# A third bank for the scores of the last batch, with its output projections two steps later

## The chip, the cores and the metric

The kernel runs on one core of one Trainium2 chip. The metric is device time in microseconds (us) of one launch. Before the change the median of three runs is 540.99 us (540.56 to 542.72).

## The reference

Input x is 8 batches of 512 tokens with 256 features. Each batch goes through one attention layer with 16 heads of 16 features:

```
xn = layer_norm(x) * norm_w + norm_b
q, k, v = xn @ q_w + q_b, xn @ k_w + k_b, xn @ v_w + v_b      (heads of 16)
att = softmax over keys of (q . k + mask term)
y   = att @ v
h   = layer_norm(y, sb weights) * (1 + scale) + shift          (scale, shift from silu(cond) @ emb_w)
out = x + silu(h) @ out_w + out_b
```

## The kernel before, in words

**Tiling.** A batch b is worked in 16 steps t: four groups of four heads (g = t // 4), and in each group four chunks of 128 keys (c = t % 4). A step computes four score tiles of 128 keys x 512 queries, one a head. Such a tile is called a unit; unit u = 4t + h. ScalarE turns a unit into probabilities with one exp (`exp_unit`, L678), and in the next step the TensorE multiplies the four probability tiles with v and accumulates them into one bank (`pv_step`, L541, 8 matmul records a step). A unit's softmax needs its query's largest score beforehand, so six steps ahead of the scores the same products are made once more the other way round (`max_quad`, L490) and reduced by VectorE (`max_pair`, L854, two reductions a step). Once every four steps the maxima of a group are turned on TensorE (`max_turn`, L500), split in two bf16 parts by VectorE (`split_max`) and written by a DMA as extra rows of q.

**PSUM.** There are eight banks: two score banks (`st_ps`), four max banks (`mx_ps`, in two pairs), one for the probability-times-v sums (`pv_ps`) and one job bank (`job_ps`). Unit h of a step takes score bank h % 2, so a score matmul waits until the exp of two units before has read its bank. In the last batch (b = 7) no maxima are due after step 9, so from step 11 on (`WIDE_STEP`) the scores take four banks: two score banks and the second pair of max banks.

**Jobs.** The rest of the work stands in tables by step. A job (`job`, written to the job bank) is a projection, a v projection or half of an output projection (`outp`) of the batch before; half A is token chunk 0 of its pair of chunks, half Z is chunk 1, and after Z VectorE adds the residual and bias (L916, reads `job_ps` and `x_res`). A side job (`side`) is four transposes into the first max bank: `yturn i` turns group i of y, `hturn i` the normalised y. It waits until VectorE has reduced the first pair of max banks in that step (`max_done`). In the last batch the job table holds only `proj 3` in step 0 (its bank is read by ScalarE, L690, in step 1) and the four outp halves.

**Order on TensorE in one step:** scores 0 and 1, max turn, pv of the step before, max matmuls, scores 2 and 3, job, side job. In the wide steps scores 2 and 3 come ahead of pv. TensorE works in this order and stops at the first instruction whose wait is not met.

**Around the end.** After the last batch comes one more body (b = 8) with only the tail: the last pv step, the last y turn, layer norm of the last y, gate and output projection (`last_rows` of each engine; TensorE fills the wait with dummy matmuls, L434). SyncE's queue (SP) handles `out` stores of the outp results (L1290) and then, in body 8, the load of `x_res`, the residual input of the last batch, 512 KB (L1278). That load waits until both outp results of batch 6 have been added (`out_ready`), as they read the same buffer. GpSimd (POOL) adds the output bias to `x_res` (L1178) and only then, in its program order, computes the reciprocal root for the last layer norm (L1095, `last_norms`), which waits for VectorE's `y_vareps` (L987), and half of the normalised rows (L1099):

```
pool.wait_ge(res_loaded, 16 * b)
pool.tensor_tensor(x_res, x_res, ob_row, ADD)     # L1178
if last_body(b):
    last_norms()                                  # L1095, L1099
```

Of the kernel before, what the change touches and what calls it, by code (L numbers as in the profile page):

```python
# [33 lines left out]
B, T, D = 8, 512, 256  # L34
# [8 lines left out]
GH = 4  # L43
NG = HEADS // GH
GC = GH * HD
STEPS = NG * CH
UNITS = STEPS * GH
# [3 lines left out]
ST_BANKS = 2  # L51
# [19 lines left out]
A, Z, AZ = (0,), (1,), (0, 1)  # L71
# [11 lines left out]
SIDE = {1: ("yturn", 3, -1), 5: ("yturn", 0, 0), 7: ("hturn", 0, -1), 9: ("yturn", 1, 0),  # L83
        11: ("hturn", 1, -1), 13: ("yturn", 2, 0)}

LAST_JOBS = {0: ("proj", 3, 0, AZ), 9: ("outp", 0, -1, A), 10: ("outp", 0, -1, Z), 11: ("outp", 1, -1, A),
             12: ("outp", 1, -1, Z)}
LAST_SIDE = {1: ("yturn", 3, -1), 5: ("yturn", 0, 0), 6: ("hturn", 0, -1), 7: ("hturn", 1, -1),
             9: ("yturn", 1, 0), 13: ("yturn", 2, 0)}
LAST_LATE = {(1, 2): ("proj", 3, 0), (7, 2): ("hturn", 0, -1), (8, 2): ("hturn", 1, -1)}  # L90

WIDE_STEP = 11

TURNS = {2: 1, 6: 2, 10: 3, 14: 4}

# [18 lines left out]
def work_at(table, b, step):  # L114

    if step not in table or not job_exists(table[step][0], b, table[step][2]):
        return None
    kind, i, db = table[step][0:3]
    return (kind, i, b + db) + table[step][3:]


def of_loop(b, first, middle, last):

    return first if isinstance(b, int) and b == -1 else last if isinstance(b, int) and b == B - 1 else middle


def wide(b, t):

    return isinstance(b, int) and b == B - 1 and t >= WIDE_STEP


def job_at(b, step):

    if step < 0:
        b, step = b - 1, step + STEPS
    return work_at(of_loop(b, FIRST_JOBS, JOBS, LAST_JOBS), b, step)

# [21 lines left out]
def exists(batch):  # L159

    return not isinstance(batch, int) or 0 <= batch < B
# [9 lines left out]
def wait(engine, semaphore, count):  # L171

    if not isinstance(count, int) or count > 0:
        engine.wait_ge(semaphore, count)
# [10 lines left out]
def attention_layer(nc, x, cond, mask, norm_w, norm_b, q_w, q_b, k_w, k_b, v_w, v_b,  # L185
                    emb_w, emb_b, sb_w, sb_b, out_w, out_b, out):
    with ExitStack() as ctx:
# [3 lines left out]
        def psum(name, shape, dt=F32):  # L191
            return ctx.enter_context(nc.psum_tensor(name, shape, dt))

        def sem(name):
            return ctx.enter_context(nc.semaphore(name))
# [68 lines left out]
        st_ps = [psum(f"st_ps{i}", [P, T]) for i in range(ST_BANKS)]  # L264
        mx_ps = [psum(f"mx_ps{i}", [P, 2, T]) for i in range(PAIRS)]
        pv_ps = psum("pv_ps", [P, T])
        job_ps = psum("job_ps", [P, T])
# [47 lines left out]
        exp_done = sem("exp_done")  # L315
# [36 lines left out]
        def emptied(kind, i, batch):  # L352
            if kind == "proj":
                return part0_ready, NG * batch + i + 1
            if kind == "yturn":
                return y_ready, NG * batch + i + 1
            of = {"xturn": xt_ready, "vproj": v_plain_ready, "hturn": h_lin_ready, "outp": out_ready}[kind]
            return of, 2 * batch + i + 1
# [9 lines left out]
        def bank_freed(t, b):  # L368

            if isinstance(b, int) and b == -1:  # L370
                return {7: (xt_ready, 1), 8: (mask_col_ready, 1)}.get(t)
            if 0 not in job_at(b, t)[3]:
                return None
            for back in range(t - 1, t - STEPS, -1):
                if isinstance(b, int) and b == 0 and back < 0:
                    return None
                job = job_at(b, back)
                if job and 1 in job[3]:
                    return emptied(*job[0:3])
            return None  # L380
# [11 lines left out]
        last_ps = [[mx_ps[i][:, k, :] for k in range(KD)] for i in range(2)]  # L392
        last_out = [job_ps, st_ps[1]]

        wide_ps = [st_ps[0][:, :], st_ps[1][:, :], mx_ps[1][:, 0, :], mx_ps[1][:, 1, :]]

        def st_bank(b, t, h):

            return wide_ps[h] if wide(b, t) else st_ps[h % ST_BANKS][:, :]

        def last_body(b):

# [26 lines left out]
        def _(pe):  # L429
# [72 lines left out]
            def st_unit(b, t, h):  # L502
                if not exists(b):
                    return
                g, c = t // CH, t % CH
                if c == 0 and h == 0:

                    pe.wait_ge(max_filled[g], 2 * 16 * (b + 1))
                    if isinstance(b, int) and b == 0 and g == 0:

                        pe.wait_ge(cond_ready, 1)
                        pe.wait_ge(part0_ready, NG - 1)

                u = GH * t + h
                if wide(b, t) and t > WIDE_STEP:
                    pe.wait_ge(exp_done, UNITS * b + u - GH + 1)
                elif wide(b, t) and h >= ST_BANKS:
                    pe.wait_ge(max_done, PAIRS * STEPS * B)
                    pe.wait_ge(max_split, NG * B)
                else:  # L520
                    wait(pe, exp_done, UNITS * b + u - ST_BANKS + 1)
                pe.matmul(st_bank(b, t, h), k_rows[0:ROWS_ALL, g, h, c * P:(c + 1) * P],  # L522
                          q_rows[0:ROWS_ALL, g, h, :], start=True, stop=True).then_inc(st_ready, 1)

# [40 lines left out]
            def job(t, b):  # L565
                if not job_at(b, t):
                    return
                kind, i, d, halves = job_at(b, t)
                ps, freed = job_bank(kind, i, b), bank_freed(t, b)
                if freed:  # L570

# [60 lines left out]
            def body(b):  # L632
                for t in range(STEPS):
                    st_unit(b, t, 0)
                    st_unit(b, t, 1)
                    max_turn(b, t)
                    if wide(b, t):
                        st_unit(b, t, 2)
                        st_unit(b, t, 3)
                    pv_step(b, t)  # L640
                    max_quad(b, t)
                    if isinstance(b, int) and b == -1 and STEPS - MAX_LEAD <= t < STEPS - 1:

                        keep_warm(st_ps[1], WARM_MAX)
                    if not wide(b, t):
                        st_unit(b, t, 2)
                        st_unit(b, t, 3)
                    job(t, b)
                    side(t, b)
                    if isinstance(b, int) and b == -1 and t == TURN_STEP:  # L650
                        turn_cond()
                    if isinstance(b, int) and b == -1 and 0 <= t - EMBEDDING_STEP < 2 * KD:
                        embedding(t - EMBEDDING_STEP)
                    if isinstance(b, int) and b == -1 and t in WARM_FIRST:
                        keep_warm(pv_ps, WARM_FIRST[t])

                if last_body(b):
                    last_rows()
# [5 lines left out]
        def _(act):  # L664
# [5 lines left out]
            def exp_unit(b, t, h):  # L670
                if not exists(b):
                    return
                u = GH * t + h
                if h == 0:

                    wait(act, pv_done, STEPS * b + t - P_SLOTS + 1)
                act.wait_ge(st_ready, UNITS * b + u + 1)
                act.activation(probs[:, t % P_SLOTS, h, :], st_bank(b, t, h), ACT.Exp).then_inc(exp_done, 1)  # L678
# [640 lines left out]
```

## Time and profile before

| | us |
|---|---|
| median of three runs | 540.99 |
| the profiled execution's own time | 541.04 |
| its span, first to last instruction | 539.3 |
| TensorE busy | 513.1 |
| VectorE busy | 414.3 |
| ScalarE busy | 367.7 |
| GpSimd busy | 193.7 |
| mean granted TensorE clock | 0.994 |

Busy times are sums over the span. Busy matmul time is modelled, so the busy share of TensorE is not how near it is to its peak. The profiled execution's time lies 1.7 us over its span.

### The profile page before, as it was taken

To read this page: it belongs to the slowest core of one execution; us is meant where nothing else is said; L and a number is where in the kernel's file an instruction comes from. 1 tells how busy PE (TensorE), PEld (TensorE's weight loads), DVE (VectorE), ACT (ScalarE), POOL (GpSimd) and SP (SyncE) were. 2 spreads that over 40 slices of the span, in tenths; PEclk is the share of its full clock that TensorE was granted. 3 is DMA by queue.
4 is the path that set the end of the run, shared out by engine and by line. 5 is a ranking of instruction groups with operands and counts; after the bars stand their busy time and mean duration, and the time that the engine had idled before them with its cause. 6 is when DMAs were issued, how large, how long until landed. Compare 5 with 4: busy or idle time off the path is not lost.

```text
span 539.3 us, 10032 instructions
## 1 busy us (share of the span) xinstructions
PE 513.1 (95%) x2840; PEld 190.4 (35%) x2843; DVE 414.3 (77%) x661; ACT 367.7 (68%) x674; POOL 193.7 (36%) x240
## 2 busy tenths in 40 slices
PE   7698999899999999999999999999999999988987
PEld 3443333233334333433333333433333333422334
DVE  6587778887887878877887878878787877877625
ACT  2205777677776788577776877677776787666761
POOL 4535213535324333425225432525225433224011
PEclk9988999999999999999999999999999999999999
DMA  5643334242425334253425333243435323252011
GB/s 132 225 117 94 91 90 127 88 135 79 136 88 159 110 104 113 60 167 92 133 86 170 103 90 118 80 157 89 127 89 163 102 84 88 79 161 55 19 61 40
DMA packets 55050, 57.95 MB, mean 107 GB/s; under 512 B 12376, under 2 KB 42200, under 8 KB 55024
## 3 DMA queue, kind: packets, MB, share of 16 engines
q1 hardware_dynamic: 54480, 56.84, 35.6%
q10 hardware_dynamic: 544, 0.79, 0.5%
q8 instruction: 12, 0.20, 0.2%
q14 instruction: 14, 0.11, 0.1%
HBM read 36.35 MB, written 21.00 MB: 106 GB/s over the span
## 4 chain that ended last, share of the span: by engine, by line
PE 75%; ACT 9%; issue 6%; DVE 4%; DMA 2%; SPq 2%; ACTq 1%; DVEq 0%; POOL 0%; POOLq 0%
PE pv_ps L541 20%; PE st_ps L522 18%; PE mx_ps L490 11%; PE job_ps L579 8%; ACT probs L678 6%; PE job_ps L586 5%; PE job_ps L599 4%; PE mx_ps L624 3%; DVE negmax L854 2%; PE mx_ps L500 2%; ACT h_tanh L726 1%; PE mx_ps L629 1%; PE st_ps L434 1%; DMA qk_dram<-qk_parts 1%; SPq L1218 1%
## 5 line engine op out<-in xcount | busy, mean ns | idle before, releaser
L854 DVE TENSOR_REDUCE negmax<-mx_ps 128x2 f32<-128x1024 f32 x256 | 303.4, 1221 | 90.5 <-PE mx_ps L490 90.4
L678 ACT ACTIVATE probs<-st_ps 128x512 f32<-128x512 f32 x502 | 273.3, 600 | 112.8 <-PE st_ps L522 111.1
L522 PE MATMUL st_ps<-q_rows,k_rows 115*128 115x512 bf16 x502 | 158.1, 385 | 6.0 <-ACT probs L678 3.4
L541 PE MATMUL pv_ps<-probs,v_rows 128*32 128x512 f32 x1024 | 136.4, 605 | 0.6 <-ACT probs L678 0.6
L1111 POOL TENSOR_TENSOR qk_rest<-qk_full,qk_parts 128x512 f32<-128x512 f32 x31 | 35.9, 1159 | 142.3 <-ACT qk_parts L690 141.9
L490 PE MATMUL mx_ps<-k_rows,q_rows 51*128 51x512 bf16 x512 | 79.4, 384 | 6.2 <-DMA k_rows<-qk_dram 4.4
L522 PEld LDWEIGHTS st_ps<-q_rows,k_rows 115*128 115x128 bf16 x502 | 38.7, 97 | 109.9 <-ACT probs L678 77.2
L1120 POOL TENSOR_TENSOR qk_parts<-qk_rest,qk_parts 128x512 bf16<-128x512 f32 x31 | 36.0, 1163 | 101.6 <-DVE qk_parts L928 99.7
L579 PE MATMUL job_ps<-x_norm_t,w_qk 128*128 128x512 f32 x116 | 59.2, 603 | 0.0
L490 PEld LDWEIGHTS mx_ps<-k_rows,q_rows 51*128 51x128 bf16 x512 | 15.8, 94 | 112.1 <-issue 54.2
L541 PEld LDWEIGHTS pv_ps<-probs,v_rows 128*32 128x32 f32 x1024 | 20.1, 108 | 33.1 <-issue 27.9
L586 PE MATMUL job_ps<-w_v,x_norm_t 128*128 128x256 f32 x120 | 31.0, 381 | 0.0
L599 PE MATMUL job_ps<-w_o,h_t 128*128 128x256 f32 x112 | 28.6, 386 | 1.0 <-DVE out_sb L916 1.0
L579 PEld LDWEIGHTS job_ps<-x_norm_t,w_qk 128*128 128x128 f32 x116 | 22.7, 196 | 11.8 <-issue 4.7
L1178 POOL TENSOR_TENSOR x_res<-x_res,ob_row 128x1024 f32<-128x1024 f32 x8 | 18.8, 2353 | 22.2 <-DMA x_res<-in_x 22.2
L698 ACT ACTIVATE qk_full<-job_ps,qkb_col 128x512 f32<-128x512 f32 x29 | 20.4, 703 | 8.5 <-PE job_ps L579 8.5
L586 PEld LDWEIGHTS job_ps<-w_v,x_norm_t 128*128 128x128 f32 x120 | 22.0, 189 | 7.3 <-ACT qk_parts L690 3.1
L1130 POOL TENSOR_TENSOR v_biased<-v_plain,vb_row 128x256 f32<-128x256 f32 x32 | 23.3, 727 | 1.1
L599 PEld LDWEIGHTS job_ps<-w_o,h_t 128*128 128x128 f32 x112 | 20.2, 189 | 9.6 <-DVE out_sb L916 3.5
L624 PE MATMUL mx_ps<-ident,y_t 128*128 128x128 f32 x128 | 19.7, 276 | 3.1 <-issue 2.1
L750 ACT COPY y_t<-pv_ps 128x512 f32<-128x512 f32 x32 | 18.8, 589 | 5.2 <-PE pv_ps L541 5.1
L1083 POOL TENSOR_TENSOR y_rstd<-y_vareps,exponent 128x4 f32<-128x4 f32 x7 | 7.1, 1019 | 40.5 <-DVE y_vareps L869 40.5
(115 smaller groups left out, 402.8 us busy)
## 6 DMA issues: line engine op xcount, KB each, us to landing
qk_dram<-qk_parts SPq DMA_DIRECT2D x128, 128.0 KB
q_rows<-qk_dram SPq DMA_DIRECT2D x124, 96.0 KB
k_rows<-qk_dram SPq DMA_DIRECT2D x124, 96.0 KB
x_in<-in_x SPq DMA_DIRECT2D x16, 256.0 KB, 3.0
x_res<-in_x SPq DMA_DIRECT2D x8, 512.0 KB, 4.0
out<-out_sb SPq DMA_DIRECT2D x16, 256.0 KB, 2.6
w_e<-in_L_cond_emb_w SPq DMA_DIRECT2D x1, 1024.0 KB, 5.9
k_rows<-mask_dram SPq DMA_DIRECT2D x64, 6.0 KB
```

The costliest lines, as they stand in the source:

```text
L490: pe.matmul(mx_ps[j][:, half, :], q_rows[base:base + ROWS_MX, g, h, c * P:(c + 1) * P], k_rows[base:base + ROWS_MX, g, h, :], start=True, ...
L522: pe.matmul(st_bank(b, t, h), k_rows[0:ROWS_ALL, g, h, c * P:(c + 1) * P], q_rows[0:ROWS_ALL, g, h, :], start=True, stop=True).then_inc(st ...
L541: mm = pe.matmul(pv_ps[VW * h:VW * (h + 1), :], v_rows[:, c, g * GH + h, :], probs[:, t % P_SLOTS, h, :], start=(c == 0), stop=(c == CH - ...
L579: mm = pe.matmul(ps, w_qk[:, k, i, :], x_norm_t[:, k, :], start=(k == 0), stop=(k == KD - 1))
L586: mm = pe.matmul(ps[:, c * D:(c + 1) * D], x_norm_t[:, k, tok:tok + P], w_v[:, k, :], start=(k == 0), stop=(k == KD - 1))
L599: mm = pe.matmul(ps[:, c * D:(c + 1) * D], h_t[:, k, tok:tok + P], w_o[:, k, :], start=(k == 0), stop=(k == KD - 1))
L624: mm = pe.transpose(ps[:, c * P:(c + 1) * P], y_t[:, c * P:(c + 1) * P], ident[:, :])
L678: act.activation(probs[:, t % P_SLOTS, h, :], st_bank(b, t, h), ACT.Exp).then_inc(exp_done, 1)
L854: dve.tensor_reduce(by_pair[:, :, j, c], mx_ps[j][:, :, :], AXIS_X, ALU.max, negate=True).then_inc(max_done, 1)
L1111: pool.tensor_tensor(qk_rest[:, :], qk_full[:, :], qk_parts[:, 0, :], ALU.subtract).then_inc(rest_ready, 1)
L1120: pool.tensor_tensor(qk_parts[:, 2, :], qk_rest[:, :], qk_parts[:, 1, :], ALU.subtract).then_inc(part2_ready, 1)
L1130: pool.tensor_tensor(v_biased[:, :, :], v_plain[:, :, g * GC:(g + 1) * GC], vb_row[:, g * GC:(g + 1) * GC].unsqueeze(1).broadcast_to((P, C ...
```

## The change

In the last batch, from step 2 to step 10, the scores take three banks in turn (score bank 0, score bank 1, job bank), so that a score matmul waits for the exp of three units before and no longer of two. To free the job bank for this, the four output projection halves of batch 6 move from steps 9, 10, 11 and 12 to steps 11, 12, 13 and 14. The first unit in the job bank waits until ScalarE has read `proj 3` out of it; the first output projection waits until the exp of unit 43, the last one in the job bank, has read it. Steps 0 and 1 and all other batches stay as they are. The number of instructions on the data is the same.

```
-LAST_JOBS = {0: ("proj", 3, 0, AZ), 9: ("outp", 0, -1, A), 10: ("outp", 0, -1, Z), 11: ("outp", 1, -1, A),
-             12: ("outp", 1, -1, Z)}
+LAST_JOBS = {0: ("proj", 3, 0, AZ), 11: ("outp", 0, -1, A), 12: ("outp", 0, -1, Z), 13: ("outp", 1, -1, A),
+             14: ("outp", 1, -1, Z)}
-WIDE_STEP = 11
+THREE_STEP, WIDE_STEP = 2, 11
+def score_bank(b, t, h):
+    if wide(b, t):
+        return (0, 1, 3, 4)[h]
+    if last_batch(b) and t >= THREE_STEP:
+        return (GH * (t - THREE_STEP) + h) % 3
+    return h % ST_BANKS
+def score_ahead(b, t, h):
+    u, bank = GH * t + h, score_bank(b, t, h)
+    if not last_batch(b) or u < ST_BANKS:
+        return u - ST_BANKS
+    of = [v for v in range(u) if score_bank(b, v // GH, v % GH) == bank]
+    return of[-1] if of else None
+def last_in_job_bank():
+    return max(v for v in range(UNITS) if score_bank(B - 1, v // GH, v % GH) == 2)
 ...
             if 0 not in job_at(b, t)[3]:
                 return None
+            if t == WIDE_STEP and last_batch(b):
+                return exp_done, UNITS * b + last_in_job_bank() + 1
 ...
-        wide_ps = [st_ps[0][:, :], st_ps[1][:, :], mx_ps[1][:, 0, :], mx_ps[1][:, 1, :]]
+        score_ps = [st_ps[0][:, :], st_ps[1][:, :], job_ps[:, :], mx_ps[1][:, 0, :], mx_ps[1][:, 1, :]]
 ...
-                if wide(b, t) and t > WIDE_STEP:
-                    pe.wait_ge(exp_done, UNITS * b + u - GH + 1)
-                elif wide(b, t) and h >= ST_BANKS:
+                ahead = score_ahead(b, t, h)
+                if ahead is not None:
+                    wait(pe, exp_done, UNITS * b + ahead + 1)
+                elif score_bank(b, t, h) == 2:
+                    pe.wait_ge(*emptied("proj", NG - 1, b))
+                else:
                     pe.wait_ge(max_done, PAIRS * STEPS * B)
                     pe.wait_ge(max_split, NG * B)
-                else:
-                    wait(pe, exp_done, UNITS * b + u - ST_BANKS + 1)
```

## Rows read from the trace of the kernel before

**Rows 1.** The page's chain that ended last, share of the span by engine.
```profile
PE 75%; ACT 9%; issue 6%; DVE 4%; DMA 2%; SPq 2%; ACTq 1%; DVEq 0%; POOL 0%; POOLq 0%
```

**Rows 2.** The same chain in order of time, steps 3 to 5: start, length, what.
```profile
482.64 0.34 PE st_ps L522
...
483.00 0.61 ACT probs L678
483.61 0.14 issue
...
484.14 0.39 PE st_ps L522
484.53 1.00 PE pv_ps L541 x8
485.53 0.54 PE mx_ps L490 x4
...
486.42 1.09 ACT probs L678 x2
```

**Rows 3.** Timeline of DVE, reductions of steps 4 and 9: start, length, line.
```profile
486.11 2.35 DVE L854 TENSOR_REDUCE negmax<-mx_ps 128x2 f32<-128x1024 f32 x2
...
504.82 2.36 DVE L854 TENSOR_REDUCE negmax<-mx_ps 128x2 f32<-128x1024 f32 x2 [0.83 <-PE mx_ps L490]
```

**Rows 4.** The chain in order of time, steps 5, 8, 9 and 10.
```profile
490.02 0.64 issue
...
502.00 1.00 ACT probs L678 x2
...
504.43 0.54 PE mx_ps L490 x4
...
505.50 0.86 PE job_ps L599 x4
506.37 0.44 PE mx_ps L624 x4
...
507.24 0.27 PE mx_ps L500
...
508.50 0.54 PE st_ps L522 x2
```

**Rows 5.** The chain in order of time, step 12 to the last pv.
```profile
514.74 1.06 PE job_ps L599 x4
515.80 0.43 PE st_ps L522 x2
...
518.73 1.92 ACT probs L678 x4
...
522.81 1.11 PE pv_ps L541 x8
```

**Rows 6.** Timelines of DVE, SP's queue and POOL (two rows) near the end.
```profile
515.84 0.69 DVE L916 TENSOR_TENSOR out_sb<-job_ps,x_res 128x512 f32<-128x512 f32 x1 [5.20 <-PE job_ps L599]
...
517.02 0.46 SPq L1278 DMA_DIRECT2D x_res<-in_x  x1
...
522.44 2.36 POOL L1178 TENSOR_TENSOR x_res<-x_res,ob_row 128x1024 f32<-128x1024 f32 x1 [22.15 <-DMA x_res<-in_x]
527.51 1.02 POOL L1095 TENSOR_TENSOR y_rstd<-y_vareps,exponent 128x4 f32<-128x4 f32 x1 [2.71 <-DVE y_vareps L987]
```

**Rows 7.** The x_res load's line: issue to landing of its eight DMAs.
```profile
DMA to landing us min/median/max: 3.4/4.0/5.4
```

**Rows 8.** Windows: length, busy PE, PEld, DVE, ACT, POOL, granted clock, DMA share, GB/s.
```profile
44.00:45.00 1.00, 0.26 (x4) 0.10 (x2) 1.00 (x2) 0.00 (x0) 0.90 (x2) 0.95 0.23 77
45.00:46.00 1.00, 1.00 (x4) 0.47 (x3) 1.00 (x2) 0.18 (x1) 1.00 (x3) 0.50 0.00 0
522.00:523.00 1.00, 0.43 (x8) 0.16 (x8) 0.00 (x0) 0.76 (x2) 0.56 (x1) 1.00 0.00 0
```

**Rows 9.** The chain in order of time, the last output projection, first half.
```profile
532.15 1.99 PE job_ps L561 x8
```

More of the change, by code:

```diff
@@ L124, in of_loop, with last_batch @@
     return first if isinstance(b, int) and b == -1 else last if isinstance(b, int) and b == B - 1 else middle
+def last_batch(b):
+    return isinstance(b, int) and b == B - 1
 def wide(b, t):
-    return isinstance(b, int) and b == B - 1 and t >= WIDE_STEP
+    return last_batch(b) and t >= WIDE_STEP
+def score_bank(b, t, h):
[12 more added lines that the diff above has]
+    return max(v for v in range(UNITS) if score_bank(B - 1, v // GH, v % GH) == 2)
 def job_at(b, step):
@@ L393, in attention_layer @@
         last_out = [job_ps, st_ps[1]]
-        wide_ps = [st_ps[0][:, :], st_ps[1][:, :], mx_ps[1][:, 0, :], mx_ps[1][:, 1, :]]
+        score_ps = [st_ps[0][:, :], st_ps[1][:, :], job_ps[:, :], mx_ps[1][:, 0, :], mx_ps[1][:, 1, :]]
         def st_bank(b, t, h):
-            return wide_ps[h] if wide(b, t) else st_ps[h % ST_BANKS][:, :]
+            return score_ps[score_bank(b, t, h)]
         def last_body(b):
```

## The prediction, made before the changed kernel was run

> **What bounds the kernel now.** I read the page's chain first: TensorE carries 75% of what ended last, ScalarE 9% [rows 1]. The change touches only the last batch, so next I read the chain in order of time from 470 us on. It has two kinds of step. In steps 2, 3, 4 and 8 the chain runs through the exps. In step 3 to 4 the reader sees score 2 of a step end at 482.98 (482.64 + 0.34), its exp start at 483.00 and end at 483.61, then 0.14 until TensorE starts again, and both next scores run before pv starts at 484.53 [rows 2]. Step 4 to 5 has the same shape: exps 1.09 long from 486.42. In steps 5, 6, 7 and 9 there is a side job, and the chain goes over VectorE: TensorE stands for 0.64 at 490.02 until the first max pair is reduced, and the two exps are done meanwhile [rows 4]. From step 11 on, with four banks, TensorE is the chain without a stop, and from 518.73 on ScalarE is, to the last pv at 522.81 [rows 5]. Behind that comes the serial tail of layer norm, gate and projection, which starts on POOL with the root at 527.51 [rows 6].
>
> **Part 1, three banks in steps 2 to 10.** pv of step t-1 needs exp 3 of that step. Between score 3 and that pv TensorE has scores 0 and 1 of step t to do. With two banks score 1 needs exp 3 as well, so after this exp comes 0.39 of a score matmul (from 484.14) and only then pv [rows 2]. With three banks score 0 needs exp 1, long done, and score 1 needs exp 2. Exp 2 ends 0.48 before exp 3 (1.09 for two, 0.61 for one), and 0.48 is about 0.14 + 0.39, so score 1 ends as exp 3 does. pv starts some 0.39 earlier. What is late next is exp 3 itself: score 2, two exps, pv and max make a ring of 0.34 + 1.09 + 1.00 + 0.54 and some 0.07 of hand-over, 3.04 us against 3.42 now. A fourth bank would give nothing more in it.
>
> This holds at four boundaries: 2 to 3, 3 to 4, 4 to 5 and 8 to 9 (there the exps from 502.00 on are late behind other ScalarE work, but pv waits for them in the same way [rows 4]). 4 x 0.39 = 1.56 us. At the boundaries behind side jobs (1, 5, 6, 7, 9) I count nothing: the exps end before the side job does.
>
> Is another engine late at the new pace? VectorE needs 2.36 a step for its reductions, plus layer norm statistics of batch 6 in steps 2 to 4. These hold the reduction of step 4 until 486.11 now, 0.58 after its max matmuls begin [rows 2, 3]. Moved by the same gains that becomes about 485.7 against 484.75 for the matmuls; it ends at 488.08, and the second max pair of step 5 is due at 488.04. So VectorE is just in time there; bounds for this term are 0.5 us lost and nothing. ScalarE has 4 exps and a copy in the ring, under 2.9 of 3.04. The new first wait of the job bank (`proj 3` read in step 1) is met a step before.
>
> **Part 2, the jobs.** Steps 9 and 10 lose a half projection of 0.86 each, steps 13 and 14 gain one of 1.06 (0.86 behind scores, 1.06 behind pv, rows 4 and 5).
> - Step 9 gives nothing back. The side job stands behind the job at 506.37, but without the job it would wait for the first of the two reductions, until about 506.1 (504.82 + 2.36 / 2 and a hand-over), and take 0.63 instead of 0.44, and the max turn behind it waits for the second reduction (504.82 + 2.36 = 507.18) and starts at 507.24 in any case [rows 3, 4].
> - Step 10, with everything 1.56 earlier: turn at 505.68, pv of step 9 at 505.95, scores to 507.49. Score 2 ends at 507.29, its exp at 507.92; score 1 of step 11 starts 0.14 later and ends at 508.45, scores 2 and 3 at 508.88, and pv of step 10 can start.
> - From here TensorE is again without a stop: four pv (4.0), four half projections (4 x 1.06), three times four scores (3 x 0.86) and the side job of step 13 (0.44) are 11.2 us. The last outp half, in step 14, ends at 520.1. In the kernel before it ends at 515.80 [rows 5]. ScalarE, with 4 exps to each such step, has time.
> - The scores of step 15 stand behind this half. Score 0 ends at 520.35, four exps take 2.06 (1.92 and more in rows 5), the last pv starts at 522.45 against 522.81. So of 1.56 won only 0.35 arrives: the two halves moved from where TensorE had the exps to wait for to where TensorE itself is the chain.
>
> **Part 3, who waits for the last outp half.** Behind it hangs a chain that had slack before: VectorE's add starts at 515.84, SP stores the result and issues the load of the last `x_res` at 517.02, it lands at 522.44 (5.42 later), POOL adds the bias until 524.80 [rows 6]. That is 9.0 us after the half ended. Behind this add, in POOL's order, stands the root of the last layer norm. It starts at 527.51, held by VectorE's `y_vareps` 0.07 earlier, so slack was 2.7 us. Now the half ends 4.3 later. The add ends at 520.1 + 9.0 = 529.1, and `y_vareps` is there at 527.1. The new stall is 2.0 us, and the root starts 1.6 later than before. Everything behind it is serial and unchanged.
>
> Bounds of this term: the eight loads of this line landed 3.4 to 5.4 after issue, median 4.0 [rows 7]. The one in question was the slowest; it goes out just behind a store of the same size in both kernels, so I take 5.4. With 3.4 the add ends at 527.1, no stall, and the kernel is 0.35 faster than before.
>
> The Trainium skill (DMA: Bandwidth & Descriptors, Anatomy of one DMA) prices a transfer on GpSimd's path at about 2 us fixed plus its bytes over 436 GB/s, which as an estimate is 3.2 us for these 512 KB. The row has 5.4; by the page's price the stall would be gone.
>
> **The sum.** Root 1.6 later: 541.04 + 1.6 = 542.6 us for an execution like the profiled one, which lies 0.05 over the median of the runs. I predict 542.6.
>
> **Rivals.**
> - *A, the load lands in time.* Speaks for it: seven of eight loads landed faster. Against: the last one has the same neighbours. At the median of 4.0 the stall shrinks to 0.6 and the time is 541.2; at 3.4 it is 540.7. This is the side on which the kernel is not slower.
> - *B, TensorE's clock falls in the tail.* Its dummy matmuls fill the wait for the normalised rows almost to its end now. They come with the last y turn, 0.35 earlier, while the rows come 1.6 later, so TensorE would stand about 2 us. The trace has both answers: the clock held through 522 to 523 with 0.43 busy, and it fell to half (1.2 GHz) at the end of 44 to 45, after two windows of 0.40 and 0.26 [rows 8]. At half clock the last projections, some 2 x 1.9 us [rows 9], and the transposes double: up to 4.3 more, about 2.5 if it comes back midway. 545.1 to 546.9. The Trainium skill (TensorE: Matmul & The Clock Gate, The HAM clock gate) says that the array goes back to half clock when it was idle and returns after sustained work; by this rule the wait is dangerous, and this case's trace agrees that such falls happen, without showing whether 2 us is enough.
> - *C, the ring doesn't shorten*, as VectorE or score 1 is late in it. Then each lost 0.39 goes straight through to the last outp half: up to 544.2.
> - *D, more is won*: the side job steps shorten too and the load is quick, 539 to 540.3. Nothing in the rows speaks for it.
>
> **Chances.** Forecast 0.52 (541.8 to 543.4), A 0.16, B 0.20, C 0.09, D 0.03. A range from 540.6 to 545.8 leaves out the upper part of B and D; the forecast's own is 541.8 to 543.4. A measurement of this kernel can tell about 0.5% from no change, which is 538.3 to 543.7. Forecast, A, and the larger part of C lie within it: same 0.74. B and the rest of C are slower: 0.24. Faster by over 0.5%: 0.02.
>
> **What would show it.** Part 1: the chain's single score of 0.39 between exp and pv gone in steps 3, 4, 5 and 9, max matmuls 3.0 to 3.1 apart, the turn of step 10 some 1.5 earlier. Part 2: last outp half ending at about 520.1, last pv at about 522.4. Part 3: the root (L1095) released by POOL's own `x_res` add and no longer by VectorE, at about 529.1, with TensorE idle for 2 us ahead of L552. Wrong if the root is still released by `y_vareps`, or if the granted clock in the last 8 us is below 1.

## The result, and the profile after

The changed kernel takes 543.25 us (median of 7 runs, 542.21 to 544.37) against 541.52 (7 runs) for the kernel before: ratio 1.0028, 95% interval 1.0015 to 1.0041. That is 1.5 us slower by the ratio (0.8 to 2.2 by its interval). The forecast, 542.6, was 1.6 over the 541.04 of the profiled execution before. The profiled execution of the changed kernel took 542.21, which is 1.2 more, and has a span of 540.5 us against 539.3. It is also the quickest of the seven. What follows finds 1.1 us in its trace; that the runs together show a little more is not explained by it.

Executions reach the last batch up to 1.4 us apart, before anything of the change is done (last section). So below I count from one event, the start of the max matmuls of step 2 in the last batch: 478.55 before, 478.67 after.

The chain that ended last, in the changed kernel, steps 3 to 5 (start, length, what), answers to [rows 2]:

```profile
482.43 0.34 PE st_ps L553
...
482.79 0.45 ACT probs L709
...
483.29 0.60 ACT probs L709
483.88 0.04 issue
483.93 1.06 PE pv_ps L572 x8
484.99 0.54 PE mx_ps L520 x4
...
486.38 0.60 ACT probs L709
486.99 0.14 issue
487.12 1.07 PE pv_ps L572 x8
```

The lone score matmul of 0.39 between exp and pv is gone; pv follows the last exp. The reader sees also what was not forecast. This pv takes 1.06 and no longer 1.00: in the last batch of these traces each pv ahead of which TensorE stands takes 1.06 to 1.11, and every other one 0.99 or 1.00. And the hand-over from exp to pv (the `issue` row) is once 0.14 and not 0.04. It is 0.14 again ahead of the pv at 502.37. Both are the first pv of a group of heads, which has two more waits in front of it in the program (`v_ready`, `yt_ready`), and the 0.14 of [rows 2] stands ahead of the first score of a group, which has one more too. That these waits cost the 0.1 fits all the rows but was not tested.

The same chain from step 9 to the last pv, answers to [rows 4, 5]:

```profile
503.43 0.54 PE mx_ps L520 x4
...
504.51 0.64 issue
...
506.23 0.28 PE mx_ps L530
...
507.87 0.61 ACT probs L709
...
519.70 1.06 PE job_ps L630 x4
520.76 0.23 PE st_ps L553
...
521.07 0.61 ACT probs L709 x2
...
523.19 1.11 PE pv_ps L572 x8
```

Step 9 starts its max matmuls 1.0 earlier than before (504.43), the last pv starts 0.4 later (522.81). The last outp half now ends at 520.76, where it ended at 515.80, and the scores of step 15 stand behind it.

Timelines of the changed kernel near the end, one engine after the other (DVE, SP's queue, POOL), answer to [rows 6]:

```profile
520.79 0.69 DVE L947 TENSOR_TENSOR out_sb<-job_ps,x_res 128x512 f32<-128x512 f32 x1 [2.21 <-PE job_ps L630]
...
527.57 0.97 DVE L1017 TENSOR_SCALAR y_negmean<-y_mv 128x4 f32<-128x4 f32 x1
528.45 0.15 DVE L1018 TENSOR_SCALAR y_vareps<-y_mv 128x4 f32<-128x4 f32 x1
...
521.97 0.46 SPq L1309 DMA_DIRECT2D x_res<-in_x  x1
...
526.16 2.35 POOL L1209 TENSOR_TENSOR x_res<-x_res,ob_row 128x1024 f32<-128x1024 f32 x1 [26.64 <-DMA x_res<-in_x]
528.69 1.02 POOL L1126 TENSOR_TENSOR y_rstd<-y_vareps,exponent 128x4 f32<-128x4 f32 x1 [0.18 <-DVE y_vareps L1018]
```

POOL's bias add on `x_res` ends at 528.51, and the root comes 0.18 behind it; before the change the add had ended 2.7 us ahead of the root. The profile names VectorE as its releaser, but look at L1017: an operation on 4 elements a partition takes 0.97 us, and the same line before took 0.17. It ends at 528.54, as the add does.

TensorE stood 1.0 us ahead of the normalised rows, from 529.56 to 530.55. The granted clock stayed at 1.00 (windows: length, busy PE, PEld, DVE, ACT, POOL, clock, DMA share, GB/s):

```profile
529.00:530.00 1.00, 0.56 (x3) 0.07 (x1) 0.26 (x1) 0.00 (x0) 0.90 (x2) 1.00 0.00 0
530.00:531.00 1.00, 0.45 (x4) 0.42 (x4) 0.65 (x2) 0.00 (x0) 1.00 (x2) 1.00 0.00 0
```

### The profile page after: what moved, and what is told of

It reads as the page before. It is cut to its first block, busy times and chain, and to the rows that moved or that the text cites. A ratio compares the mean times of both kernels' runs of the same rounds, so it can differ in the third digit from the quotient of the medians.

```text
span 540.5 us, 10035 instructions
## 1 busy us (share of the span) xinstructions
PE 515.2 (95%) x2843; PEld 190.8 (35%) x2843; DVE 414.9 (77%) x661; ACT 367.2 (68%) x674; POOL 193.5 (36%) x240
## 4 chain that ended last, share of the span: by engine, by line
PE 72%; ACT 9%; issue 9%; DVE 4%; POOL 3%; SPq 1%; DMA 1%; ACTq 0%; DVEq 0%; POOLq 0%
PE pv_ps L572 20%; PE st_ps L553 17%; PE mx_ps L520 10%; PE job_ps L610 7%; ACT probs L709 6%; PE job_ps L617 5%; PE job_ps L630 4%; PE mx_ps L655 3%; ACT h_tanh L757 1%; PE mx_ps L530 1%; DVE negmax L885 1%; PE mx_ps L660 1%; SPq L448 1%; PE pv_ps L464 1%; PE job_ps L623 1%
## 5 line engine op out<-in xcount | busy, mean ns | idle before, releaser
L709 ACT ACTIVATE probs<-st_ps 128x512 f32<-128x512 f32 x490 | 267.2, 600 | 111.7 <-PE st_ps L553 110.4
L553 PE MATMUL st_ps<-q_rows,k_rows 115*128 115x512 bf16 x490 | 154.3, 384 | 4.2 <-ACT probs L709 1.8
L610 PE MATMUL job_ps<-x_norm_t,w_qk 128*128 128x512 f32 x116 | 58.0, 592 | 0.0
```

The costliest lines, as they stand in the source:

```text
L610: mm = pe.matmul(ps, w_qk[:, k, i, :], x_norm_t[:, k, :], start=(k == 0), stop=(k == KD - 1))
```

## The experiments

All with the kernel before on the same chip. The last three columns are us in the profiled execution, the first two of them counted from the max matmuls of step 2.

| kernel | ratio to before (95%) | last pv starts | root starts | L1017 takes |
|---|---|---|---|---|
| before | 1 | 44.26 | 48.96 | 0.17 |
| changed | 1.0028 (1.0015 to 1.0041) | 44.52 | 50.02 | 0.97 |
| three banks only, steps 2 to 8 | 0.9994 (0.9981 to 1.0007) | 43.38 | 48.08 | 0.17 |
| jobs moved only | 1.0047 (1.0029 to 1.0066) | 46.12 | 51.60 | 0.95 |
| changed, early residual | 1.0007 (0.9995 to 1.0019) | 44.53 | 49.23 | 0.17 |
| before, early residual | 1.0005 (0.9992 to 1.0018) | 44.25 | 48.95 | 0.17 |
| changed, root first on POOL | 1.0023 (1.0009 to 1.0036) | 44.54 | 49.24 | 0.17 |
| changed, add twice | 1.0069 (1.0049 to 1.0088) | 44.53 | 52.19 | 1.04 |
| three banks, steps 2 to 9 | 0.9974 (0.9961 to 0.9987) | 43.15 | 47.85 | 0.17 |

L1017 is the operation `y_negmean` in the last body; its line number differs from kernel to kernel.

**Three banks only.** The projections stay in steps 9 to 12, and steps 9 and 10 use two banks.

```
-LAST_JOBS = {..., 11: ("outp", 0, -1, A), 12: ..., 13: ..., 14: ("outp", 1, -1, Z)}
+LAST_JOBS = {..., 9: ("outp", 0, -1, A), 10: ..., 11: ..., 12: ("outp", 1, -1, Z)}
+TWO_STEP = 9        # from here banks 1, 0, 1, 0; from step 11 on banks 1, 0, 3, 4
```

> Three banks in steps 2 to 8 only; the output projections stay in steps 9 to 12 as before, steps 9 and 10 use two banks. Theory: the three-bank ring wins about 0.28 at each of four boundaries (1.1 in all, as the changed kernel's max matmuls of step 9 show, 503.43 against 504.43 from a start 0.1 later), and with the projections in their old place all of it reaches the last pv and the last outp half: 1.1 us faster than before, ratio 0.998, last pv at about 521.7, root released by VectorE with POOL idle. Rival (what the ring wins is given back behind, by side jobs, ScalarE or VectorE, whatever the projections do): ratio 1.000, last pv at 522.8.

The last pv and the root each come 0.88 earlier. Three boundaries of the ring win here, and nothing of it is given back. The fourth, from step 8 to 9, does not win, as step 9 is back to two banks. POOL's add is done 3.7 us before the root:

```profile
521.20 2.36 POOL L1211 TENSOR_TENSOR x_res<-x_res,ob_row 128x1024 f32<-128x1024 f32 x1 [21.16 <-DMA x_res<-in_x]
527.27 1.02 POOL L1128 TENSOR_TENSOR y_rstd<-y_vareps,exponent 128x4 f32<-128x4 f32 x1 [3.70 <-DVE y_vareps L1020]
```

So the theory's place holds, and 0.88 of its 1.1 was there. Over all runs the ratio can't be told from 1. Times follow the mean granted clock of the whole execution (last section), and among runs with the same clock the gain shows: 540.1 (2 runs) against 541.1 (7) at 0.994, 540.9 (4) against 541.9 (12) at 0.991, 542.1 (4) against 543.3 (3) at 0.987. More of this kernel's runs than of the other's happened to have a low clock.

**Jobs moved only.** The kernel before, with the four halves in steps 11 to 14 and two banks.

```
-LAST_JOBS = {..., 9: ("outp", 0, -1, A), 10: ..., 11: ..., 12: ("outp", 1, -1, Z)}
+LAST_JOBS = {..., 11: ("outp", 0, -1, A), 12: ..., 13: ..., 14: ("outp", 1, -1, Z)}
```

> Two banks as before, only the four output projection halves in steps 11 to 14. Theory: no ring gain, so the last outp half ends about 1.1 later than in the changed kernel, at 521.9, the last pv starts at about 524.3, the x_res add ends some 7.8 behind the half, at 529.7, and the root starts there, 2.3 us later than before: ratio 1.004. Rival (moving the projections costs nothing by itself, the loss comes with the third bank): ratio 1.000.

The last pv comes 1.86 later and the root 2.64, both relative to before. The theory holds against its rival, but its 524.3 for the last pv came out at 524.86 and its 2.3 at the root at 2.6. The third bank pays 1.60 of the 1.86 back at the last pv: 1.12 up to the max matmuls of step 9, and 0.48 at one boundary more, from step 10 to 11, which the theory had left out. There, with the projections gone, TensorE waits for the exps again, for two of them here (1.09) and for one in the changed kernel (0.61, at 507.87). The extra 0.8 at the root is again the residual add: it ends at 530.16, and the root follows 0.18 behind (chain of this kernel, then one row of POOL's timeline):

```profile
509.04 1.09 ACT probs L678 x2
...
521.36 1.06 PE job_ps L599 x4
...
524.86 1.11 PE pv_ps L541 x8
...
529.24 0.04 DVE y_negmean L986
529.28 0.82 issue
530.10 0.17 DVE y_vareps L987
...
527.81 2.35 POOL L1178 TENSOR_TENSOR x_res<-x_res,ob_row 128x1024 f32<-128x1024 f32 x1 [27.35 <-DMA x_res<-in_x]
```

**Changed, early residual, and its control.** The last batch's residual input gets a buffer of its own, loaded in the middle of the last batch, in the changed kernel and in the kernel before.

```
+x_last = sb("x_last", [P, CH, D])
 spread(b, 3, 0)
+if last_batch(b):
+    sp.dma_start(x_last[:, :, :], batch_of(x_dram, b)).then_inc(last_loaded, 16)
 # body 8: no x_res load; POOL adds the bias to x_last, the last adds read x_last
```

> The changed kernel, with the last residual input in a buffer of its own that is loaded in the middle of the last batch, so that POOL's bias add is done 25 us before the root. Theory: VectorE's two small operations ahead of the root (L1017, L1018) take 0.17 each again and end 4.0 us or so after the last pv ends minus 0.5, the root starts 0.8 us earlier: ratio to before 1.0006, to the changed kernel 0.9985. Rival (the 0.85 in front of y_vareps has nothing to do with the x_res add, it is VectorE's own): it stays, ratio to before 1.002.

> The kernel before with the same early load in a buffer of its own, as a control. Theory: the add had 2.7 us of slack in the kernel before, so nothing changes: ratio 1.000 within 0.1%. Rival (the load or the add near the end costs something also in the kernel before, for instance by slowing DMAs or VectorE): 0.3 us or more faster, ratio 0.9995 or less.

In the changed kernel both small operations are short again and the root starts 0.79 earlier:

```profile
527.48 0.17 DVE L1019 TENSOR_SCALAR y_negmean<-y_mv 128x4 f32<-128x4 f32 x1
527.55 0.16 DVE L1020 TENSOR_SCALAR y_vareps<-y_mv 128x4 f32<-128x4 f32 x1
...
527.80 1.02 POOL L1128 TENSOR_TENSOR y_rstd<-y_vareps,exponent 128x4 f32<-128x4 f32 x1 [26.06 <-DVE y_vareps L1020]
```

In the kernel before nothing moves (44.25 and 48.95, against 44.26 and 48.96). The residual chain costs the changed kernel 0.8 us and the kernel before nothing.

**Changed, root first.** Is it POOL's order, or VectorE held by the add?

```
+if last_body(b):
+    last_norms()
 pool.wait_ge(res_loaded, 16 * b)
 pool.tensor_tensor(x_res, x_res, ob_row, ADD)
-if last_body(b):
-    last_norms()
```

> The changed kernel with POOL's order turned in its last body: root and normalised rows first, the bias add on x_res behind them. Theory 1 (VectorE operations that read two SBUF operands, or fp32 SBUF to SBUF in the fast form, stand still while POOL works on SBUF): the root starts 0.8 us earlier, at about 527.9, but the 2.35 us add now runs from about 530.3 to 532.6 and holds up VectorE's h_t (L1038), which stretches from 0.69 to 1.5 or more, so little or nothing is won: ratio to before 1.002 to 1.0025. Theory 2 (only POOL's order cost the time, and the long negmean operation was a bystander): h_t stays at 0.69 and the whole 0.8 is won: ratio 1.0007.

Timelines of POOL and DVE:

```profile
530.52 2.34 POOL L1211 TENSOR_TENSOR x_res<-x_res,ob_row 128x1024 f32<-128x1024 f32 x1
...
532.07 1.34 DVE L1038 SCALAR_TENSOR_TENSOR h_t<-h_tanh,h_lin 128x512 f32<-128x512 f32 x1 [0.24 <-ACT h_tanh L812]
533.34 0.98 DVE L1034 TENSOR_SCALAR h_lin<-mx_ps,mod_now 128x256 f32<-128x256 f32 x2
534.56 0.69 DVE L1038 SCALAR_TENSOR_TENSOR h_t<-h_tanh,h_lin 128x512 f32<-128x512 f32 x1 [0.24 <-ACT h_tanh L812]
```

The root starts 0.78 earlier, and 0.65 of it is lost again in h_t, on which the last projection waits: 1.34 while the add runs to 532.86, 0.69 the next time. The ratio, 1.0023, can't be told from the changed kernel's. Theory 1 holds in kind: h_t is stretched while POOL's add runs, if to 1.34 and not to the 1.5 or more that it named. A bare change of order wins 0.1 us of the 0.8.

**Changed, add twice.** A second add of the same size ahead of the root.

```
+if last_body(b):
+    pool.tensor_tensor(x_spare, x_in, ob_row, ADD)
     last_norms()
```

> The changed kernel with a second bias add of the same size (from x_in into a spare tile) behind the first, ahead of the root on POOL. POOL's order alone puts the root at about 530.9, 2.3 later: ratio to before 1.007. Theory 1 (VectorE waits for POOL's hold on SBUF): VectorE's negmean operation (L1017), issued at about 527.6, ends only as one of the adds does, at 528.5 or at 530.9, so it takes 1.0 or 3.3 us. Theory 2 (its 0.97 us came from elsewhere): it takes 0.17 or 0.97 wherever the adds end.

```profile
528.28 1.04 DVE L1018 TENSOR_SCALAR y_negmean<-y_mv 128x4 f32<-128x4 f32 x1
...
526.95 2.35 POOL L1210 TENSOR_TENSOR x_res<-x_res,ob_row 128x1024 f32<-128x1024 f32 x1 [26.72 <-DMA x_res<-in_x]
529.25 2.34 POOL L1213 TENSOR_TENSOR x_spare<-x_in,ob_row 128x1024 f32<-128x1024 f32 x1
531.56 1.01 POOL L1127 TENSOR_TENSOR y_rstd<-y_vareps,exponent 128x4 f32<-128x4 f32 x1
```

Negmean ends at 529.32, beside the end of the first add (529.30), and gets its turn between the two adds. So the hold lasts for one instruction. The second add goes through to the root by POOL's order alone, as VectorE was ready by 529.4; the root comes 2.2 later than in the changed kernel (52.19 against 50.02). TensorE now stood from 530.28 to 533.42, and here the clock did fall, to half (1.2 GHz):

```profile
533.00:534.00 1.00, 0.58 (x5) 0.44 (x5) 0.51 (x2) 0.03 (x1) 0.93 (x2) 0.97 0.00 0
534.00:535.00 1.00, 1.00 (x6) 0.94 (x6) 0.79 (x2) 0.69 (x2) 0.00 (x0) 0.50 0.00 0
535.00:536.00 1.00, 1.00 (x4) 0.34 (x3) 0.76 (x2) 0.87 (x2) 0.00 (x0) 0.50 0.00 0
536.00:537.00 1.00, 1.00 (x3) 0.49 (x2) 1.00 (x3) 0.31 (x1) 0.00 (x0) 0.50 0.00 0
537.00:538.00 1.00, 1.00 (x5) 0.87 (x4) 0.74 (x2) 0.25 (x1) 0.00 (x0) 0.82 0.00 0
```

The price was small: from the root to the end of the span 12.5 us (531.56 to 544.1) against 11.8 in the changed kernel, 0.7 more. The half clock fell mostly on the transposes (1.68 us for 1.23) and the dummy matmuls (2.34 for 1.24), and it was nearly over when the last projections started at 537.02.

**Three banks to step 9, jobs in their old steps.** What the two halves of the change suggest together.

```
+THREE_STEP, JOB_STEP, WIDE_STEP = 2, 9, 11
+    if last_batch(b) and THREE_STEP <= t <= JOB_STEP:
+        return (GH * (t - THREE_STEP) + h) % 3
+            if t == JOB_STEP and last_batch(b):      # the first outp half waits for the exp of unit 37
+                return exp_done, UNITS * b + last_in_job_bank() + 1
```

> Three banks in turn from step 2 to the end of step 9, two in step 10, and the four output projection halves in their old steps 9 to 12. The half in step 9 waits for the exp of unit 37 (score 1 of step 9), over long before. Theory (ring gain at four boundaries and no cost at the jobs): from the max matmuls of step 2 to the last pv 43.1 us, against 44.26 before and 43.38 in the kernel with three banks to step 8 only; the x_res chain keeps its slack, the root is released by VectorE with POOL idle. Ratio 0.998 if programs start alike. Rival (only the boundaries up to step 5 win): 43.4 and 0.9984.

```profile
478.50 0.67 PE mx_ps L520 x4
...
503.26 0.54 PE mx_ps L520 x4
504.34 0.86 PE job_ps L630 x4
...
521.65 1.11 PE pv_ps L572 x8
```

It is faster than the kernel before, and so than the changed one: ratio 0.9974 (0.9961 to 0.9987), median 540.04 us, last pv and root each 1.11 earlier than before, as the theory had it. All four boundaries win and nothing is given back.

**Both kernels once more**, a second profile of each.

> The kernel before once more, for a second profile of it. In the first one the last x_res load took 5.42 us from issue to landing, in four changed kernels 4.2 to 4.5. If the load's length is set by the kernel (what else the queues carry there), it is 5.4 again; if it varies from one execution to the next, about 4.2 to 4.5. The last pv starts 44.2 to 44.3 us behind the max matmuls of step 2 and the root 48.9 to 49.0 behind, in either case.

> The changed kernel once more, for a second profile. Theory (the x_res add ends behind VectorE's negmean operation and holds it): the add ends some 3.0 us behind the last outp half's store is issued plus its landing, negmean (L1017) starts about 4.4 us behind the last pv's start and takes as long as the add is still running, so 0.6 to 1.3 us with a load of 4.2 to 4.5, up to 2.2 with one of 5.4. The last pv 44.5 behind the max matmuls of step 2.

Last pv and root: 44.25 and 48.95 for the kernel before, 44.53 and 49.87 for the changed one, each within 0.15 of the first profile. Negmean took 0.81 this time. The load of `x_res` took 4.78 in the kernel before and 4.04 in the changed one, so neither alternative held: with the job in its old step it was 5.42, 4.78, 4.42 and 4.75, with the job late 4.0 to 4.3 in five profiles. It varies, and it was shorter at the later place in all of these. Why is open.

## Why the prediction was right, step by step

The sign and the place were right. The size was right in part by luck, as two errors have opposite signs. The last pv was forecast 0.6 us too early, mostly because the ring won less, and the stall 1.2 us too long, because the load came sooner than assumed. With only the first put right, the same sum would have given about 543.2; with only the second, about 541.4, which is outside the forecast's own range.

- **Part 1, the ring.** Forecast 1.56 for four boundaries, measured 1.12 to the max matmuls of step 9 (25.88 to 24.76 from those of step 2): spacings of 3.22, 3.10 and 3.20 against 3.56, 3.42 and 3.42 give 0.34, 0.32 and 0.22, the last boundary the rest. The mechanism was right, the term mis-sized: 0.07 a step because pv behind a stand takes 1.06, and 0.1 at the last two, where the hand-over was 0.14 and not 0.04. VectorE was in time, as worked out (its reductions of step 4 ended at 488.25, and the second pair of max matmuls of step 5 was due at about 488.5), and the boundaries behind side jobs won nothing, as forecast.
- **Part 2, the jobs.** Step 9 gave nothing back, as forecast (the 0.64 wait at 504.51 takes the job's place). From the max matmuls of step 9 to the end of the last outp half 17.33 us against 17.23 forecast. With the smaller ring gain the half ended at 520.76, not 520.1, and the last pv started at 523.19, not 522.45: 0.26 later than before from the common event, where 0.35 earlier was forecast. The last sentence of that part, that the halves moved from where TensorE waits to where it is the chain, is what the jobs-only kernel shows with 1.86 us. That three banks also shorten the wait from step 10 to 11, as this part had worked out, is the 0.48 us by which the jobs-only kernel is behind there.
- **Part 3, the residual chain.** Shown by the early-residual kernel to cost 0.8 us, where 2.0 was forecast. The step that was mis-sized is the load: I took 5.42 us, the slowest of eight, and it took 4.19, so the add ended 7.75 behind the half and not 9.0. The median of [rows 7], 4.0, was the better value.
- **How it costs.** I had POOL's order alone. The add also holds VectorE, and by the letter my own sign of being wrong came true: the root is still released by `y_vareps`. The prediction did not foresee this. It is not the sign of a missing stall that I took it for, as the early-residual kernel takes 0.8 us away and the long negmean with it. With POOL's order as it is, the second way added at most 0.2: the root starts 0.18 behind the end of the add here and in the jobs-only kernel, and with no gap behind the second add in the doubled one, where VectorE was long ready. But it is why turning the order wins next to nothing.
- **The sum.** From the common event 0.26 at the last pv and 0.80 at the root make 1.06; with a start 0.12 later that is 528.69 against 527.51. Forecast was -0.35 and 2.0.
- **Rival A**: its ground, a quicker load, did come about, and its price for a load of 4.0, a stall of 0.6, was near the measured 0.8. Its time of 541.2 did not, because the ring won less. **Rival B** did not occur: TensorE stood 1.0 us and not 2, and the clock held. With the doubled add it stood 3.1 us and the clock fell, at a price of 0.7, where 2.5 to 4.3 had been estimated; what 2 us would do no run shows. **Rival C** is where the smaller ring gain belongs. **Rival D** did not occur in this kernel.

## What to carry to other kernels

A job can be free in one step and cost its full length a few steps later: what counts is whether the engine has something to wait for there, and a change that frees a bank by moving work should look for the last step in which both fit (here the bank up to step 9, the work in steps 9 to 12). Follow moved work to whoever waits behind it off the main chain, down to loads that reuse its buffer, and count their slack. And where a small VectorE operation on the critical tail is long, look for a POOL operation that ends with it, whatever releaser the profile names.

## What was not expected of the hardware

- Some VectorE operations stood still beside a POOL add of 2.35 us: negmean (SBUF to SBUF, fp32, one tensor) took 0.97, 0.81, 0.95 and 1.04 us for 0.17, and h_t (two tensors from SBUF) 1.34 for 0.69. Operations that read PSUM were not longer beside it (h_lin, the pair 1.00, with the add from 530.52 to 532.86), nor were the layer norm statistics, which read one tensor from SBUF (L1007, four in 0.60 from 526.47, with the add from 526.16 to 528.51; 0.60 before). The Trainium skill (SBUF — State Buffer, Who interferes with whom) says that VectorE and GpSimd share one pair of SBUF ports under an exclusive lock, which `tensor_scalar` in its fast form needs, and operations with two SBUF inputs beside a GpSimd operation that reads SBUF, and that the loser blocks for the whole instruction. This case's traces agree in which operations were held and which not, and in the release between two adds; that it is a lock on ports is the Trainium skill's account, a trace shows only the lengths. The effect was to be seen in the trace of the kernel before, and the prediction had passed it over. There the same small operation of the other layer norm (L868) is long again and again, and ends as a POOL operation does: 405.53 and 405.50 in these two rows of the timelines of DVE and POOL. Seven of 15 took 0.21 to 0.57, each ending within 0.03 us behind a POOL operation, and the other eight, with POOL idle, 0.17.

```profile
404.96 0.57 DVE L868 TENSOR_SCALAR x_negmean<-x_mv 128x4 f32<-128x4 f32 x1
...
404.78 0.72 POOL L1130 TENSOR_TENSOR v_biased<-v_plain,vb_row 128x256 f32<-128x256 f32 x1
```

- The kernel before came to the max matmuls of step 2 of its last batch at 478.55 in one execution and at 479.98 in another. The two windows from 20 to 50 us, of the kernel before and of its second profile:

```profile
20.00:50.00 30.00, 23.34 (x117) 10.99 (x118) 21.90 (x40) 5.63 (x10) 14.64 (x19) 0.89 0.38 116
...
20.00:50.00 30.00, 25.01 (x114) 11.34 (x113) 22.94 (x41) 4.86 (x9) 15.97 (x20) 0.85 0.39 115
```

  The granted clock there was 0.89 and 0.85, and a lower clock went with a later start. The timed runs show the same over whole executions. In the two rounds of experiments the kernel before took 540.79 to 541.53 us at a mean granted clock of 0.993 or 0.994 (27 runs), 541.47 to 542.74 at 0.991 (16) and 542.68 to 543.72 at 0.987 (8). So most of the scatter of the times goes with the clock, and runs at one clock are the ones to compare. Why an execution gets one or another was not tested.
